# A recurrence whose scan inputs are multiplied on VectorE out of PSUM instead of on GpSimd out of a copy

## What is computed

```python
ph = jnp.exp(-(re * re + im * im)) * jnp.exp(1j * jnp.arctan2(im, re))
prog = jnp.power(ph[None, :], jnp.arange(length)[:, None])
filt = prog * pinit[None, :]
conv = ifft(fft(filt, n=2 * length) * fft(x, n=2 * length))[:, :length, :]
return (conv + last * prog[None, :, :] * ph[None, None, :]).real
...
h = h + _L1_attn_ref(_layernorm(h, axis=-1), ...)
h = h + _L1_ffn_ref(_layernorm(h, axis=-1), ...)
```

## Time and profile before

| | |
|---|---|
| median of 3 runs | 1924.59 us (1922.29 to 1925.28) |
| the profiled execution's own time | 1914.82 us |
| its span, first to last instruction | 1913.0 us |
| the recurrence in it | about 1551 to 1666 us from the span's start |
| mean granted TensorE clock over the span | 0.906 |

### The profile page before, as it was taken

One profiled execution on the slowest core, in us unless ns is written; L12 is line 12 of the kernel. 1 busy time (PEld: TensorE's weight loads), 2 busy tenths in 40 slices (PEclk: granted clock), 3 DMA queues, 4 the chain that ended last, 5 costly groups with the idle time before them and its releaser, 6 DMA issues. The chain is left out here.

```text
span 1913.0 us, 32335 instructions
## 1 busy us (share of the span) xinstructions
PE 1589.7 (83%) x11205; PEld 1476.6 (77%) x11205; DVE 1221.8 (64%) x2397; ACT 1011.1 (53%) x2168; POOL 1055.0 (55%) x827
## 2 busy tenths in 40 slices
PE   7749898989898989897728999999999926698329
PEld 4338898989898989897628999999999915598219
DVE  6756565656565656564643666666655549658896
ACT  3536564656564656563615555555555524448562
POOL 0486767676767676762355776676777736300000
PEclk9869998999998999999558999999999957799659
DMA  5153000000000000000336555555555521103123
GB/s 192 65 176 118 1 8 0 8 0 8 0 8 0 8 0 8 0 9 4 107 109 214 142 138 147 139 138 143 143 145 144 149 75 33 33 1 118 66 75 114
DMA packets 74599, 142.85 MB, mean 75 GB/s; under 512 B 7400, under 2 KB 50728, under 8 KB 73992
## 3 DMA queue, kind: packets, MB, share of 16 engines
q1 hardware_dynamic: 63992, 127.80, 21.5%
q0 software_dynamic: 10512, 13.83, 4.2%
HBM read 108.15 MB, written 46.83 MB: 81 GB/s over the span
## 5 line engine op out<-in xcount | busy, mean ns | idle before, releaser
L1463 POOL TENSOR_TENSOR expert_w_low<-expert_raw,expert_w_high 128x768 fp32r<-128x768 f32 x152 | 289.5, 1958 | 157.6 <-ACT expert_w_high L1322 156.7
L646 ACT ACTIVATE probs<-psum,neg_max 120x376 f32<-120x376 f32 (+2 forms) x384 | 176.4, 479 | 140.1 <-DVE neg_max L763 140.1
L716 POOL TENSOR_TENSOR qk_low<-rotated,qk_high 128x376 fp32r<-128x376 f32 x128 | 138.3, 1081 | 180.2 <-ACT qk_high L639 175.9
L533 PE MATMUL psum<-diag,probs 128*128 128x128 f32 (+2 forms) x1536 | 203.5, 283 | 26.9 <-DVE pt_low L779 22.7
L533 PEld LDWEIGHTS psum<-diag,probs 128*128 128x128 f32 (+2 forms) x1536 | 185.5, 194 | 36.2 <-issue 25.5
L779 DVE TENSOR_TENSOR pt_low<-psum,pt_high 128x752 fp32r<-128x752 f32 x128 | 120.5, 941 | 142.5 <-ACT pt_high L655 141.5
L1439 DVE TENSOR_TENSOR expert_act_low<-expert_act,expert_act_high 128x384 fp32r<-128x384 f32 x152 | 148.6, 977 | 79.6 <-ACT expert_act_high L1360 79.6
L1360 ACT ACTIVATE expert_act_high<-expert_act 128x384 fp32r<-128x384 f32 x152 | 79.8, 525 | 171.4 <-DVE expert_act L1434 171.4
L1281 PE MATMUL psum<-slots_high,expert_w_high 128*128 128x384 f32 x608 | 157.9, 340 | 9.0 <-DVE expert_act L1434 7.8
L1281 PE MATMUL psum<-slots_low,expert_w_high 128*128 128x384 f32 x608 | 155.3, 336 | 0.0
L1281 PE MATMUL psum<-slots_high,expert_w_low 128*128 128x384 f32 x608 | 155.1, 336 | 0.0
(11 more groups left out here) (303 smaller groups left out, 4549.4 us busy)
## 6 DMA issues: line engine op xcount, KB each, us to landing
expert_raw<-in_experts SPq DMA_DIRECT2D x152, 384.0 KB, 3.1
x_slots<-in_c_slots SPq DMA_DIRECT2D x4, 3168.0 KB, 27.9
slot_rows<-x_slots SPq DMA_DIRECT2D x19, 396.0 KB, 4.8
up_spill<-held SPq DMA_DIRECT2D x5, 1128.0 KB, 4.9
held<-up_spill SPq DMA_DIRECT2D x5, 1128.0 KB, 5.7
patch<-in_patches SPq DMA_DIRECT2D x4, 752.0 KB, 6.8
hid_spill<-hid SPq DMA_DIRECT2D x1, 3008.0 KB, 8.5
resid<-hid_spill SPq DMA_DIRECT2D x8, 376.0 KB, 3.5
```

Of the source, the lines that this page charges most:

```text
L533: last = pe.matmul(psum[0:nj, BANK_PT + bank, at:at + ni], probs[0:ni, h % 2, src:src + nj], diag[0:ni, h % 2, it, 0:ni], start=True, stop ...
L646: last = act.activation(probs[0:ni, h % 2, at:at + P * it + ni], score_bank(h % 2, it), ACT.Exp, bias=neg_max[0:ni, h % 2, it:it + 1], acc ...
L716: pool.tensor_tensor(qk[1][:, c % 2, k, :], rotated[:, k, :], qk[0][:, c % 2, k, :].bitcast(F32), ALU.subtract).then_inc(qk_ready, 1)
L1463: pool.tensor_tensor(w[1][:, g % RING, :], raw[:, g % RAW, :], w[0][:, g % RING, :].bitcast(F32), ALU.subtract).then_inc(w_low, 1)
```

## The change

The tile `late_xt` and ScalarE's keep(b) are gone. feeding(b, k) moves from GpSimd to VectorE and reads the turned rows in their banks. On VectorE, feeding(0, ...) stands before the loop and feeding(i+1, ...) between inverse2(i-2) and peak(i-3) of turn i; on GpSimd only the turn-backs remain. turn_x(b) waits for feeding(b-1, 1) instead of for the copy, and in TensorE's turn it now stands behind turn_y(i-2).

```diff
@@ TensorE: turn_x
                     pe.wait_ge(x_made, b + 1)
                     if b:
-                        pe.wait_ge(xt_kept, b)
+                        pe.wait_ge(fed_im, b)
...
@@ TensorE: the loop
                     if here(i - 1):
                         join(i - 1)
+                    if here(i - 2):
+                        turn_y(i - 2)
                     if here(i + 2):
                         turn_x(i + 2)
-                    if here(i - 2):
-                        turn_y(i - 2)
...
@@ ScalarE
-                def keep(b):
-                    act.wait_ge(x_turned, b + 1)
-                    if b >= 2:
-                        act.wait_ge(fed_re, b - 1)
-                        act.wait_ge(fed_im, b - 1)
-                    act.activation(xt[:, b % 2, :, :], psum[:, BANK_X:BANK_X + 2, 0:TOK], ACT.Copy).then_inc(xt_kept, 1)
...
@@ VectorE
+                def feeding(b, k):
+                    u = b % 2
+                    dve.wait_ge(x_turned, b + 1)
+                    dve.tensor_tensor(fed[:, u, k, :, :], psum[:, BANK_X:BANK_X + 2, 0:TOK], feed[:, k, :, :],
+                                      ALU.mult).then_inc((fed_re, fed_im)[k], 1)
...
                 inverse(1)
+                for k in range(2):
+                    feeding(0, k)
...
                     if here(i - 2):
                         inverse2(i - 2)
+                    if here(i + 1):
+                        for k in range(2):
+                            feeding(i + 1, k)
                     if here(i - 3):
                         peak(i - 3)
...
@@ GpSimd
-                def feeding(b, k):
-                    u = b % 2
-                    pool.wait_ge(xt_kept, b + 1)
-                    if b >= 2:
-                        pool.wait_ge(scanned, 2 * (b - 2) + k + 1)
-                    pool.tensor_tensor(fed[:, u, k, :, :], xt[:, u, :, :], feed[:, k, :, :],
-                                       ALU.mult).then_inc((fed_re, fed_im)[k], 1)
...
-                for b in range(2):
-                    feeding(b, 0)
-                    feeding(b, 1)
                 for i in range(BATCH):
                     for k in range(2):
                         turn_back(i, k)
-                        if here(i + 2):
-                            feeding(i + 2, k)
```

More of the change, by code:

```diff
@@ L1499, in recurrence @@
         shift = sb("late_shift", [P, 2, T])
-        xt = sb("late_xt", [P, 2, HALVES, TOK])
         fed = sb("fed", [P, 2, 2, HALVES, TOK])
@@ L1513, in recurrence @@
         stored = [sem(f"rec_stored{u}") for u in range(2)]
-        (summed, std_made, rstd_made, x_made, x_turned, xt_kept, fed_re, fed_im, scanned, turned_back, join_made, join_kept,
+        (summed, std_made, rstd_made, x_made, x_turned, fed_re, fed_im, scanned, turned_back, join_made, join_kept,
          summed2, std2_made, rstd2_made, y_made, y_turned, norm_kept, peak_made, step, prepared) = (
             sem(f"rec_{n}") for n in
-            "summed std_made rstd_made x_made x_turned xt_kept fed_re fed_im scanned turned_back join_made join_kept "
+            "summed std_made rstd_made x_made x_turned fed_re fed_im scanned turned_back join_made join_kept "
             "summed2 std2_made rstd2_made y_made y_turned norm_kept peak_made step prepared".split())
@@ L1649, in _ @@
                     normalise(b)
-                    keep(b)
                 for i in range(BATCH + 2):
@@ L1659, in _ @@
                         keep_join(i - 1)
-                    if here(i + 2):
-                        keep(i + 2)
                     if here(i - 2):
```

## The result

| | before | changed |
|---|---|---|
| median | 1924.59 us (5 runs, 1922.29 to 1927.02) | 1914.62 us (5 runs, 1909.39 to 1916.32) |
| profiled execution | 1914.82 us | 1916.32 us |
| ratio, 95% interval | | 0.9942 (0.9922 to 0.9962) |

A forecast was written before the change was run, and what follows sets the result against it. VectorE was taken to bound the loop, with about 3.1 us a turn held up by GpSimd. Head 6.5 plus loop 4.7 minus tail 0.2 gave 11.0 us off, 1924.6 to 1913.6 us; range 1905 to 1920.

The forecast's parts named there:

- A: Rival: last_shift gets its operand before turn_back(b, 1), so (d) costs nothing; 1906 to 1909.6 us; chance 20%.
- B: Rival: joins bound the loop, which keeps 11.8 us turns, or TensorE stays at 1.2 GHz; 1918 to 1921 us; chance 15%.
- C: Rival: VectorE's products, held beside GpSimd's turn-back, take 1.8 instead of 0.9 us; kernel ends at 1928 us; chance 5%.
- (a): Part 1 scans on VectorE: GpSimd idle when they start, so the pair falls from 4.89 us to 1.81.
- (b): ScalarE's wait for the turned rows goes; late_std's lateness for VectorE, 0.29 us a turn, is taken off.
- (c): Two new products a batch on VectorE, one operand in PSUM: 1.80 us a pair; bounds 0.88 and about 1.8 each.
- (d): last_shift, right behind scan(b, 1), is held by GpSimd's turn_back(b, 1): 1.6 us a turn, for batches 2 to 7.
- The turn: One loop turn on VectorE sums to 11.32 us against 11.8; five turns 54.3 against 59.0, a gain of 4.7.
- The joins: In the loop, join(b-2) is done 7 to 8 us into the next turn; slack about 3 us, no wait left.
- The head: First scan to the scan of batch 2: scan(2, 0) starts at 1578.4 instead of 1584.9, gaining 6.5 us.
- The tail: From scan(7, 0) to the end of join(7): 13.95 us against 13.8, costing 0.2; 3 more at half clock.

The follow-up runs named there:

- e5: Kernel before, with GpSimd's products of batches 2 to 7 cut to the first 8 of 376 tokens; stage 101.6 us against 115.3.
- e1: Changed kernel with the two products moved ahead of inverse2 on VectorE; stage 94.5 us against 103.2, ratio 0.9897 to the kernel before.
- e4: e2 with ScalarE's copy of the turned rows back and VectorE's products reading it; stage 107.1 us against e2's 94.4.
- e9: Changed kernel with last_shift made by three 128x1 instructions, each with one tensor operand and a pointer; stage 94.5 us against 103.2.
- e3: Changed kernel with turn_x ahead of turn_y again on TensorE; stage 103.8 us against 103.2.
- e6: Changed kernel with one more 128x512 reduction on VectorE in each of turns 0 to 7; stage 108.4 us against 103.2.
- e2: e1 with turn_x ahead of turn_y again on TensorE; stage 94.4 us against e1's 94.5, ratio 0.9890 to the kernel before.
- e12: e1's kernel again, timed in rounds beside e9's; 1893.48 us against 1913.96 of the kernel before, ratio 0.9894, stage 94.7 us.
- e8: Changed kernel, unchanged, traced a second time; stage 101.6 us against 103.2 in its first trace, tail 22.4 against 24.0.

## Why the prediction was right

The forecast was 11.0 us off; the medians gave 10.0, the ratio 11.2, the stage 12.2 to 15.0. All rivals fell: `last_shift` is held (against A), the loop lost 6.1 us and its waits for joins (against B), the products are not held (against C). The new bound and its terms were right. What bounds the loop before was read too simply, without harm to the sum. The prediction takes VectorE's queue for the bound and the joins for a wait of five times; they came last in every turn. The sum compares a new queue with the measured 59.0 us, so it did not need the old bound. Also, GpSimd is not quite idle beside the first pair of scans: its 2.02 us product of turn 4 starts at 1609.86, while that pair runs until 1610.30. Point by point:

- **(a) Held scans.** The pair of part 1 takes 1.89 us in turns 0 to 5 and 2.31 in turns 6 and 7, as said. e5 shows the cause, GpSimd's work beside the scans.
- **(b) ScalarE's wait** is gone; the rows of the turn have no bracket.
- **(c) The product** took 914 to 942 ns against the 880 to 940 that I had bounded it with, and 1.70 us a pair from start to start where I used 1.80. In turns 0 and 1 the pair of products runs beside a turn-back, and in e1 in every turn, without a hold. e4 is what it would have cost with both operands in SBUF, so the lower bound was the right one for the right reason.
- **(d) The block that moves into the open** came in six of eight, at 1.76 us each. Rival A would have had VectorE first; GpSimd was first by 0.02 us all six times. e1 puts its price at 1.6 us a turn. e9 saves 1.3 us, since its added instructions cost 0.3. A's own price, 4 to 8 us for a loop without the hold, was about right: e1 got 7.7 of the loop.
- **The turn.** 10.98 us against 11.32. No term failed, four were some 0.1 us too large: products 1.70, peak 0.92, inverse 0.25, stat and stat2 2.63. The peak's 1.00 had held 0.08 us of waiting, for the join that ended at 1619.59. So the loop gained 6.1 to 6.7 instead of 4.7.
- **The joins.** No wait for them is left, as forecast. The slack, put at about 3 us, is 2.4 to 5.1 in the loop. Rival B is out by e3 and e6 too.
- **The head** gained 7.6 to 8.4 instead of 6.5. The step that was off is join(0), put down at 6.6 us of half clock. TensorE in the changed kernel's head, from turn_x(2), the first and last row of join(0), and VectorE's scan(2, 0):

```profile
1583.87 1.49 PE L1550 MATMUL psum<-ident,late_x 128*128 128x128 f32 x6 [5.84 <-DVE fed L1686]
1585.15 0.65 PE L1563 MATMUL psum<-ident,state 128*128 128x128 f32 x2
...
1590.07 0.60 PE L1566 MATMUL psum<-late_h,ident 120*120 120x256 f32 x2
```

```profile
1591.05 1.95 DVE L1695 TENSOR_TENSOR_SCAN state<-decay,vectors,fed 128x376 f32<-128x376 f32 x2
```

The join took 5.5 us, since the granted clock rose to full at 1588.0 inside it; scan(2, 0) then started at once behind the products, 26.3 us into the stage. In the time of the first trace that is 1577.3, just where the sum had put VectorE (1577.4) and a microsecond ahead of the join's 1578.3. In the runs whose head is 26.8 to 27.1 us (e1, e2, e3, e9, e12) the join was the later one.

- **The tail** was forecast to cost 0.2, and 3 more with TensorE at half clock. It cost 1.6 in the first trace and nothing in the second. The turn_y ahead of join(7) and the last row of that join, in the first trace of the changed kernel:

```profile
1652.91 1.51 PE L1577 MATMUL psum<-ident,last_x 128*128 128x128 f32 x6 [4.55 <-ACT last_x L1630]
...
1658.75 0.60 PE L1566 MATMUL psum<-late_h,ident 120*120 120x256 f32 x2
```

and in its second trace, e8:

```profile
1649.95 0.87 PE L1577 MATMUL psum<-ident,last_x 128*128 128x128 f32 x6 [2.41 <-ACT last_x L1630]
...
1654.19 0.60 PE L1566 MATMUL psum<-late_h,ident 120*120 120x256 f32 x2
```

5.84 us at a clock that was half until 1656.3, and 4.24 at full clock: the difference of 1.6 us is the difference of the two tails. In e6, where the half clock lasted longer, the tail is 2.7 us above 22.4, near the 3 that the prediction had for it.

- **From stage to total.** The stage says 12 to 15 us, the ratio 11.2 with an interval of 7 to 15. The two agree, and the timed runs alone could not have told 11 from 13. So the forecast was 1 to 4 us short of the stage's gain; that it lies within a microsecond of the medians is in part luck. For the profiled execution it had put 1903.8 us, and that took 1916.32: the stage's gain was there, but the execution shown of before had been the quick one ahead of it.

## What to carry to other kernels

When a small operation, or a scan, takes several times its usual time, look at what GpSimd does in the same microseconds before counting anything as work of VectorE. Moving work from GpSimd to VectorE need not load VectorE more, when it ends such a hold and the moved operation reads one operand from PSUM: here VectorE's busy time in the stage fell from 90.9 to 85.9 us, with sixteen products more to do. And put behind the event that starts GpSimd what can't be held, the product out of a bank, and not what can: here the order of two steps was worth another 7 to 9 us of the stage, beside the 12 to 15 of the change. And compare when an operand is ready with when its reader starts: a wait too short for a bracket in the rows can still be the one that ends last.

## What the runs showed that was not expected

- How much the holds had cost: taking GpSimd's products away, with everything else in place (e5), freed 11.8 of the loop's 59.0 us, although VectorE's rows had shown it 88% busy.
- The joins came last in every turn of the loop before: all six ended 0.11 us ahead of their scan, in both traces, though only four of the loop's five scans had a wait in brackets.
- An operation on three elements paid 1.6 us in six of eight turns, and a pointer to a value per partition in place of the second tensor (e9, 0.20 to 0.22 us an instruction) was never held.
- A stage some 530 us ahead of the change's place ran 110 us at half clock in one execution, and 120 and 123 in the two others shown. That is as much as the whole change, and hid it in the comparison of the two profiled executions.
- The kernel before had medians between 1914 and 1927 us from one set of runs to the next, so each ratio here is within its set.
